# Two load buffers, two store buffers and counts of their own in the weight preparation of a hybrid attention and ternary FFN kernel

## What is computed

```
x = x + attn_a(layernorm(x))     # differential attention, Wproj 2048 x 2048, gate
x = x + ffn(layernorm(x))        # both matrices ternary
x = x + attn_b(layernorm(x))     # causal attention with relative bias rpb
x = x + ffn(layernorm(x))        # same weights again
```

```
def weight_quant(w):
    scale = 1.0 / clip(mean(abs(w)), 1e-5)
    return clip(round(w * scale), -1, 1) / scale
w1: 4096 x 1024    w2: 1024 x 4096
attn_b: w = softmax(q k / sqrt(d) + bias), bias[h,i,j] = rpb[j - i + 2047, h], causal
```

## Time and profile before

| | us |
|---|---|
| runs, median of 2 | 21759.46 |
| lowest, highest | 21719.41, 21799.51 |
| profiled execution, its own time | 21871.0 |
| its span, slowest core (5) | 21869.3 |
| spans of the other cores | 21535.9 to 21866.1 |

### The profile page before, as it was taken

The page is one execution under the profiler, slowest core; times in us unless marked ns, Lnnn a source line. Parts: engine busy times, 40 slices in busy tenths (PEclk is TensorE's granted clock), DMA queues, the critical chain, the costliest instruction groups (busy, mean ns, idle before and its releaser), DMA issues.

```text
span 21869.3 us, 103330 instructions; the slowest of 8 cores (21535.9 to 21869.3 us)
## 1 busy us (share of the span) xinstructions
PE 9424.7 (43%) x36356; PEld 3356.4 (15%) x36356; DVE 7917.2 (36%) x6352; ACT 4969.9 (23%) x3978; POOL 119.5 (1%) x228
## 2 busy tenths in 40 slices
PE   1125556554243345523334555556432334543333
PEld 0002121121111111101111121121111111111111
DVE  1134222223444444454444322222344444444443
ACT  2311434432011022211100234434110012221100
POOL 0000000000000000000000000000000000000000
PEclk7556878877666667766666778877666666676666
DMA  3220000000121200002121000000011210001122
GB/s 129 71 85 9 2 4 2 2 4 12 22 45 32 40 19 16 16 17 46 32 38 53 6 4 2 2 4 2 19 28 34 41 37 16 16 14 29 32 40 55
DMA packets 1313257, 591.26 MB, mean 27 GB/s; under 512 B 1140090, under 2 KB 1272442, under 8 KB 1303418
## 3 DMA queue, kind: packets, MB, share of 16 engines
q1 hardware_dynamic: 1297786, 532.14, 10.5%
q0 software_dynamic: 14976, 52.51, 0.6%
HBM read 532.07 MB, written 52.49 MB: 27 GB/s over the span
## 4 chain that ended last, share of the span: by engine, by line
DVE 24%; PE 24%; ACT 18%; DMA 12%; DVEq 7%; issue 6%; PEldq 5%; PEld 2%; ACTq 1%; SPq 0%; POOL 0%; POOLq 0%
ACT Ebuf_s L1009 9%; PE ps L1627 5%; PE ps L979 4%; DMA tchDF_s_s<-t_c 2%; DMA tchDD_s_s<-t_c 2%; DVEq L1520 2%; DVE scr_s L1018 2%; DVEq L1020 2%; ACT EbufE_s L1953 2%; PE ps L1458 1%; PE ps L1462 1%; PE ps L947 1%; DMA wchunk<-w2T 1%; DVE scr2DF_s_s L1518 1%; DVE scr2DD_s_s L1518 1%
## 5 line engine op out<-in xcount | busy, mean ns | idle before, releaser
L1009 ACT ACTIVATE Ebuf_s<-ps,consts 128x1024 bf16<-128x1024 f32 x2048 | 2285.8, 1116 | 1427.0 <-PE ps L982 1425.5
L1018 DVE RECIPROCAL scr_s<-ps 128x512 f32<-128x512 f32 x128 | 429.8, 3358 | 4144.2 <-PE ps L1001 4144.2
L979 PE MATMUL ps<-QT_s,KT_s 32*128 32x512 bf16 x2048 | 872.9, 426 | 1887.8 <-ACT Ebuf_s L1009 886.4
L1627 PE MATMUL ps<-k2bF_s_s,tchDF_s_s 128*128 128x512 bf16 x2048 | 589.4, 459 | 750.7 <-DVEq L1592 486.5
L1627 PE MATMUL ps<-k2bD_s_s,tchDD_s_s 128*128 128x512 bf16 x2048 | 580.5, 454 | 748.9 <-DVEq L1592 487.0
L982 PE MATMUL ps<-QT_s,KT_s 32*128 32x512 bf16 x2048 | 898.7, 439 | 0.0
L1181 PE MATMUL ps<-TT_s,wpj_s 128*128 128x512 bf16 x2048 | 497.8, 409 | 846.0 <-DMA c3s_s<-xt 804.6
L988 PE MATMUL ps<-Ebuf_s,ones 128*128 128x512 bf16 x1920 | 832.1, 433 | 0.0
L989 PE MATMUL ps<-Ebuf_s,ones 128*128 128x512 bf16 x1920 | 823.4, 429 | 0.0
L990 PE MATMUL ps<-Ebuf_s,Vp_s 128*128 128x512 bf16 x1920 | 817.1, 426 | 0.0
L1953 ACT ACTIVATE EbufE_s<-ps,consts 128x1024 bf16<-128x1024 f32 x640 | 714.4, 1116 | 450.6 <-PE ps L1939 449.8
(11 more groups left out here) (395 smaller groups left out, 17135.3 us busy)
## 6 DMA issues: line engine op xcount, KB each, us to landing
tchDD_s_s<-t_c SPq DMA_DIRECT2D x256, 256.0 KB, 3.7
tchDD_s_s<-t_c SPq DMA_DIRECT2D x128, 512.0 KB, 6.0
tchDF_s_s<-t_c SPq DMA_DIRECT2D x256, 256.0 KB, 3.7
tchDF_s_s<-t_c SPq DMA_DIRECT2D x128, 512.0 KB, 6.0
wchunk<-w1T SPq DMA_DIRECT2D x16, 2048.0 KB
wchunk<-w2T SPq DMA_DIRECT2D x64, 512.0 KB
wchunk<-ZB SPq DMA_DIRECT2D x16, 1280.0 KB
expAB_s<-expb_c SPq DMA_DIRECT2D x32, 640.0 KB
```

Of the source, the lines that this page charges most:

```text
L979: t.matmul(ps[:, SA:SA + 512], z.KT[r0:r0 + 32, kcol:kcol + 128], z.QT[r0:r0 + 32, qcol:qcol + 512], start=True, stop=True, tile_position= ...
L1009: s.activation(Ebuf[:, eb:eb + 1024], ps[:, 0:1024], AF.Exp, bias=z.consts2[:, s_i - 1:s_i]).then_inc(sA.h, 1); sA.n += 1
L1018: v.reciprocal(scr[:, 0:512], ps[:, ZA:ZA + 512])
L1627: last = t.matmul(ps[:, 1024 + pb:1024 + pb + 512], tch[:, hidx * 2048 + c * 128:hidx * 2048 + (c + 1) * 128], k2b[:, hc * QW:(hc + 1) * Q ...
```

## The change

Lines of the changed kernel shift by up to 63. Semaphores `dX0`, `dX1` (loads, already there and used by the later phases) and the new `dY0`, `dY1` (stores) count by parity of the chunk. Loads alternate between `wchunk` and `wchunk2`, stores between `bchunk` and the new `bch4` (`bch3` for ZB). Abs works in place. The two Signs write to the new bf16 tiles `sg1` and `sg2`; the sum reads these and writes bf16, and the factor 0.5 is applied in place in bf16. Exp writes bf16 into `sg1` or `sg2`. `z.ldtok[p]` holds the count at which buffer p is free: the last reader's. `_quiesce` waits for `dY0` and `dY1` too.

```diff
+    z.sg1 = ... [128, 4096], BF16      # sg2, bch4 alike; bch3 [128, 2560]
...
     cache_weight:
+            buf = (z.wchunk, z.wchunk2)[p]
+            outb = (z.bchunk, z.bch4)[p]
             sync:
-                wt(q, sV)
-                wt(q, dL)
-                q.dma_start(out=z.wchunk[:, 0:cols], in_=src[...]).then_inc(dL.h, 16)
+                s_, v_ = z.ldtok[p]
+                wt(q, s_, v_)
+                q.dma_start(out=buf[:, 0:cols], in_=src_t[...]).then_inc(dXk.h, 16)
             vector:
-                wt(v, dL)
-                wt(v, dS)
+                wt(v, dXk, tok_l)
+                wt(v, dYk, 16 * store_cnt[p])
...
     tern_weight, first pass:
             scalar:
-                wt(s, dL)
-                wt(s, sT)
-                s.activation(z.wchunk2[:, 0:cols], z.wchunk[:, 0:cols], AF.Abs)
+                wt(s, dXk, tok_l)
+                s.activation(buf[:, 0:cols], buf[:, 0:cols], AF.Abs)
             tensor:
-                wt(t, sA)
+                wt(t, sA, tok_a)
+            z.ldtok[p] = (sT, sT.n)
...
     tern_weight, second pass:
             sync:
-                wt(q, sA)
-                wt(q, sV)
-                wt(q, dL)
+                if r0i < 2:
+                    wt(q, sV, tok_red)
+                s_, v_ = z.ldtok[p]
+                wt(q, s_, v_)
             scalar:
-                wt(s, dL)
-                wt(s, sG)
-                wt(s, sV)
-                s.activation(z.wchunk2[:, 0:cols], z.wchunk[:, 0:cols], AF.Sign, ...)
+                wt(s, dXk, tok_l)
+                if r0i == 0:
+                    wt(s, sG, tok_sg)
+                if r0i >= 1:
+                    s_, v_ = add_toks[-1]
+                    wt(s, s_, v_)
+                s.activation(z.sg1[:, 0:cols], buf[:, 0:cols], AF.Sign, ...)
                 s.drain()
-                s.activation(z.wchunk[:, 0:cols], z.wchunk[:, 0:cols], AF.Sign, ...)
+                s.activation(z.sg2[:, 0:cols], buf[:, 0:cols], AF.Sign, ...)
+            z.ldtok[p] = (sA, sA.n)
             vector:
-                wt(v, dS)
-                v.tensor_tensor(z.wchunk2, z.wchunk2, z.wchunk, ALU.add)
+                wt(v, dYk, 16 * store_cnt[p])
+                v.tensor_tensor(outb, z.sg1, z.sg2, ALU.add)
                 v.drain()
-                v.tensor_scalar(z.bchunk, z.wchunk2, 0.5, None, ALU.mult)
+                v.tensor_scalar(outb, outb, 0.5, None, ALU.mult)
+                v.drain()
...
     ZB, per head:
             scalar:
-                wt(s, dL)
-                wt(s, sV)
-                s.activation(z.wchunk2[:, 0:2560], z.wchunk[:, 0:2560], AF.Exp)
+                wt(s, dXk, tok_l)
+                s_, v_ = mul_toks[p]
+                wt(s, s_, v_)
+                s.activation(sgb[:, 0:2560], buf[:, 0:2560], AF.Exp)
```

More of the change, by code:

```diff
@@ L418, in _ @@
             g.drain().then_inc(sG.h, 1); sG.n += 1
-        for r0 in range(0, rows, 128):
+        tok_sg = sG.n
+        add_toks = [(sV, tok_red)]
+        store_cnt = [dY[0].n // 16, dY[1].n // 16]
+        for r0i in range(nch):
+            r0 = r0i * 128
+            p = r0i % 2
+            buf = bufs[p]
+            dXk, dYk = z.dX[p], dY[p]
             @blk.sync
             def _(q):
[L422 to L425, removed]
+                if r0i < 2:
+                    wt(q, sV, tok_red)
+                s_, v_ = z.ldtok[p]
+                wt(q, s_, v_)
+                q.dma_start(out=buf[:, 0:cols], in_=srcT[r0:r0 + 128, :]).then_inc(dXk.h, 16); dXk.n += 16
+            tok_l = dXk.n
@@ L426, in _ @@
             @blk.scalar
             def _(s):
[L428 to L431 removed]
+                wt(s, dXk, tok_l)
[4 more added lines that the diff above has]
+                    wt(s, s_, v_)
+                s.activation(z.sg1[:, 0:cols], buf[:, 0:cols], AF.Sign,
                              bias=z.consts[:, 0:1], scale=z.consts[:, inv_col:inv_col + 1])
@@ L440, in _ @@
-                wt(v, dS)
-                v.tensor_tensor(z.wchunk2[:, 0:cols], z.wchunk2[:, 0:cols], z.wchunk[:, 0:cols], ALU.add)
+                wt(v, sA, tok_s2)
+                wt(v, dYk, 16 * store_cnt[p])
+                v.tensor_tensor(outb[:, 0:cols], z.sg1[:, 0:cols], z.sg2[:, 0:cols], ALU.add)
                 v.drain()
-                v.tensor_scalar(z.bchunk[:, 0:cols], z.wchunk2[:, 0:cols], 0.5, None, ALU.mult).then_inc(sV.h, 1); sV.n += 1
+                v.tensor_scalar(outb[:, 0:cols], outb[:, 0:cols], 0.5, None, ALU.mult)
@@ L450, in _build_body @@
     tern_weight(w2T, t2_c, 4 * E, E, E * 4 * E, 10, 12)
+    mul_toks = [(sV, sV.n), (sV, sV.n)]
+    store_cnt = [dY[0].n // 16, dY[1].n // 16]
     for h in range(16):
+        p = h % 2
+        buf = (z.wchunk, z.wchunk2)[p]
+        sgb = (z.sg1, z.sg2)[p]
+        outb = z.bchunk[:, 0:2560] if p == 0 else z.bch3[:]
+        dXk, dYk = z.dX[p], dY[p]
         @blk.sync
         def _(q):
-            wt(q, sA)
-            wt(q, sV)
-            wt(q, dL)
-            q.dma_start(out=z.wchunk[:, 0:2560], in_=ZBin[h]).then_inc(dL.h, 16); dL.n += 16
+            s_, v_ = z.ldtok[p]
+            wt(q, s_, v_)
+            q.dma_start(out=buf[:, 0:2560], in_=ZBin[h]).then_inc(dXk.h, 16); dXk.n += 16
+        tok_l = dXk.n
@@ L468, in _ @@
-            v.tensor_tensor(z.bchunk[:, 0:2560], z.wchunk2[:, 0:2560], z.maskf[:], ALU.mult).then_inc(sV.h, 1); sV.n += 1
+            wt(v, sA, tok_e)
+            wt(v, dYk, 16 * store_cnt[p])
+            v.tensor_tensor(outb, sgb[:, 0:2560], z.maskf[:], ALU.mult).then_inc(sV.h, 1); sV.n += 1
+        mul_toks[p] = (sV, sV.n)
+        tok_m = sV.n
         @blk.gpsimd
         def _(g):
-            wt(g, sV)
-            g.dma_start(out=expb_c[h], in_=z.bchunk[:, 0:2560]).then_inc(dS.h, 16); dS.n += 16
+            wt(g, sV, tok_m)
+            g.dma_start(out=expb_c[h], in_=outb).then_inc(dYk.h, 16); dYk.n += 16
@@ L474, in _build_body @@
+        store_cnt[p] += 1
     prep_es.close()
```

79 lines of the change are left out of this document (56 added, 23 removed).

## The result

| | us |
|---|---|
| before, median of 10 runs | 21738.98 |
| after, median of 11 runs | 21255.71 |
| lowest, highest after | 21167.46, 21321.15 |
| after / before, 95% interval | 0.977, 0.974 to 0.980 |
| profiled execution of after, its own time | 21336.54 |

The change makes the kernel 483 us faster by these medians (before and after were run side by side), and 534.5 by the two profiled executions (21871.0 - 21336.5). The forecast was 21224 by the median and 21335.4 for the profiled execution. The interval of the ratio lies at the edge of the 2% that a measurement of this kernel can tell from no change. The 483 is less than the preparation gave up; the experiments show what scatters the time of the whole kernel by more than that difference.

The account below looks back on a forecast made before the run. It took the preparation (1337.9 us) for a relay through single buffers and the rest as unchanged. Stage terms fell from 1317.6 to 782.0 us, saving 535.6: 21759.5 - 535.6 = 21223.9 us, range for 8 in 10 21110 to 21370.

Parts of the forecast that it names:

- rival C: After the preparation: changed TensorE clock puts the slowest core 666.8 us further behind, kernel slower at 21891 us; chance 0.02.
- Bound (d): Preparation stages: DMA bytes over rate set the turn, 5.24 us in the cast of Wproj, 6.28 in ZB.
- The estimates of 72 and 96 us: Cast of Wproj and ZB priced by the skill's 358 GB/s: 4.4 and 5.5 us a turn, 25 us less in all.
- The added wait: Sign passes: ScalarE waits for the previous chunk's VectorE work, so only the load is hidden; turns 13.1 and 5.47 us.
- my choice and the lower end: Sign passes: the bf16 scale halves as the add did, to 1.2 us for w1 and 0.43 for w2.
- rival B: Preparation gives more: full-clock matmuls in Abs passes, Sign turns bound by loops; saving 596 us, time 21164; chance 0.20.
- My low ends for matmuls at full clock: Abs passes: matmuls of 7 us a chunk for w1 and 1.7 for w2, making the stages 84 and 133 us.
- A: Preparation gives less: transfers at 222 GB/s, lower TensorE clock, slower w2 loads, unchanged scale; saving 407 us, time 21353; chance 0.10.
- D: Preparation: loads do not run ahead, only 16-bit adds and scales gain, 51 us; time 21708; chance 0.02.

Follow-up runs that it names:

- the second experiment: Changed kernel with a single load buffer in the two Sign passes; preparation 915.3 us against 789.7 in the changed kernel.
- the first four experiments: Changed kernel with, in turn: second pair of Sign tiles, one load buffer in Sign passes, f32 Sign tiles, third store buffer; preparation 738.9, 915.3, 826.2, 790.6 us.
- the single blocks: Changed kernel with ScalarE's loop over the chunks in one program block per pass, not one per chunk; preparation 703.5 us, one kernel run 21165.69 us.
- the last experiment: Changed kernel unedited, measured again beside the kernel before: 21338.95 us (6 runs) against 21877.87 (11 runs), ratio 0.9752.

## Why the prediction was right

**What bounds the kernel.** Right for the preparation: it was a relay, and with two buffers and 16-bit tiles 550 us of it went. Incomplete for the rest. I read 333.4 us between cores 5 and 6 as a matter of TensorE's clock, and gave it to rival C, "all but a few us of it" in the later part. In the trace of before 21 of them are in the preparation (1335.9 against 1314.7 us), and 290 are the FFN passes, of which core 5 has four long ones and core 6 none.

**The sum, term by term** (the stages' rows above):

| | predicted | measured |
|---|---|---|
| first load issued | 20.3 | 18.4 |
| cast of Wproj | 85 | 83.9 |
| Abs and sum of w1 | 92 | 93.8 |
| reductions | 24.4, 24.6 | 24.6, 25.9 |
| Sign of w1 | 110 | 108.3 |
| Abs and sum of w2 | 160 | 155.0 |
| Sign of w2 | 178 | 172.1 |
| exp of ZB | 108 | 105.5 |
| preparation ends | 802.3 | 787.5 |

- *Cast and ZB.* Bound (d), bytes over rate, was the right one of the four. The third store buffer took 2.7 us from the cast and nothing from ZB, and 1.28 us less in the loop of ZB's load buffer took 0.1 us from its turn and not 0.64. The rate was right for the cast, 304 GB/s at 0.91, where I had scaled 222 at 0.74 up to 300. For ZB I had 313 and its middle moved 328, so the turn was 5.96 against 6.28. Whether a second load in flight adds rate these rows leave open: one load and one store moved 222 GB/s in a stretch that was not full, at 0.74, two of each 304 at 0.91. The estimates of 72 and 96 us by the Trainium skill's 358 GB/s beside a streaming neighbour (HBM Reference, Specifications (TRN2)) did not come, the stages took 83.9 and 105.5: with loads and stores mixed these stretches moved 304 and 328 GB/s, and the 354 of the earlier trace rows were loads alone.
- *Sign passes.* The added wait keeps ScalarE and VectorE in series, as the prediction said; the second pair of tiles took 50.8 us out by removing it. The turns are 12.86 and 5.34 against 13.1 and 5.47: all links together are 0.46 us where I had 0.7 and 0.59, which over 31 turns is 4 of the 5.9 us by which the w2 pass was over-priced. The scale cost 1.23 and 0.427, my choice and the lower end; the f32 tiles show the add's share to be 34 us, as 8 x (4.43 - 2.29) + 32 x 0.53 gives.
- *Abs passes.* The w1 pass is 1.8 us over the forecast. In the w2 pass the clock granted to TensorE was 0.73 instead of 0.60, so that its matmuls took 89.50/32 = 2.8 us a chunk instead of 3.4. This was the direction of rival B, at a small part of its size. My low ends for matmuls at full clock, 7 and 1.7 us, do not follow from the rows: if the time goes as the clock, 8.8 us at 0.86 make 7.6 and 3.4 at 0.60 make 2.0, and the measured 8.1 at 0.91 and 2.8 at 0.73 give 7.4 and 2.0. The second load buffer's price in the Sign passes, 125.6 us, was too high by 23 in my expectation of the second experiment, where a load of w2 turned out at 3.6 us and not 4.6.
- *The rest.* 20547.5 us, within the 150 that I allowed around 20531. That the profiled execution came within 1.1 us of its forecast (21336.5 against 21335.4) is luck: the preparation was 14.8 us under the sum and the rest 16.1 over, on a core that had other long passes than the slowest of before. The mean over the cores went from 20309 to 20390 in these two traces, with long passes in 8 of 32 before and in 10 of 32 after. Of the 81 us, 42 lie in the FFN passes and 39 outside them; what those 39 are stays open, since the six traces of the other kernels with the small stores (the first four experiments, the single blocks, the changed kernel once more) are within 17 us of before outside the FFN. These six had 24, 18, 18, 10, 14 and 14 long passes. The one trace of before happened to have few: the mean of its cores' spans is 21644 us, 121 under the 21764 of the 11 runs of before in the last experiment, and there the change took 555 us from the mean, with a standard error of 22. So nothing shows that the change makes pairs fall into step more often.

**The rivals.** A (transfers at 222 GB/s, a slow scale) falls by 304 and 328 GB/s and 427 ns. D falls by the chain of the Sign passes, which has no load in it. B asked for 60 us beyond the forecast; the preparation ended 14.8 under the sum, 5 of them in the pass where TensorE's clock rose. C did not happen, but its place was real and its mechanism wrong: the small stores choose the slowest core. The 32 us between the forecast and the median of 21255.71, like the 83 us between that median and the one of the last experiment, are well inside what they do, a long pass being 75 to 85 us; that they are the cause of either was not shown.

## What to carry to other kernels

In a relay of single buffers, price each stage after the change by its four bounds (loop of a load buffer, loop of a store buffer, serial engines, bytes over the rate that a mixed stretch of the trace shows), and look at which is longest: here it was the rate in two stages and the new wait in two others, and a third store buffer where the rate binds bought 2.7 us of 84 and nothing. The last wait in the chain does not tell the loop of a buffer from the rate: shorten the loop and see whether the transfers get longer. Before comparing whole times, ask why the cores of one execution differ: here 300 us between them had a cause of its own, and its removal was worth nearly as much as the change (21857.9 - 21379.4 = 478.5 us). A block per chunk costs a table load per chunk; keep an engine's loop in one block where that engine sets the turn.

## What was not expected of the hardware

- Four stores of 128 x 4 bytes from POOL's queue to DRAM took 6.5 us each from issue to landing, 9 to 10 us in the passes that the neighbouring core had begun within some 10 us, and a single one of 128 x 16 bytes 1.7 us. With eight such groups per pass, a D pass took about 1825 and 1900 us, and 1770 with the single stores. The Trainium skill's advice to coalesce many small transfers (DMA: Bandwidth & Descriptors, Rules for kernel authors) is borne out.
- Two cores that disturb each other in this way fall into step: they mostly leave the pass less than 4 us apart after having begun it up to 10 us apart, and the one that began earlier pays for it.
- Loads and stores together moved 304 GB/s in 60 us of the cast, at a DMA share of 0.91, and 328 in 70 us of ZB, at 0.95, where loads alone had moved 354 at 0.92.
- A load of 2.1 MB took 8.2 us in the median at a DMA share of 0.61 in its pass, and 11.8 where the second pair of Sign tiles had brought the transfers closer together, at 0.76.
